# Router logits from the beta and output products of a delta-rule attention layer, with a new order of the calls in its loops

## The reference

```python
x = L0_attn_x                                   # (8, 512, 256)
x = x + attn(layernorm(x), ...)                 # 4 heads, dk 128, dv 64
x = x + ffn(layernorm(x), router_w, w1, w2)     # 8 experts, top 2, hidden 1024

# attn: q, k, v, g = x@Wq, x@Wk, x@Wv, x@Wg; beta = sigmoid(x@Wb); k normalised; q scaled
#   S_t = S_{t-1} + k_t (beta_t (v_t - k_t^T S_{t-1}))^T ;  o_t = q_t^T S_t
#   o = rms_norm(o) * norm_w * silu(g);  return o @ Wo
# ffn: probs = softmax(x @ router_w.T); the best two experts of each row
#   out = sum over the two of prob * (gelu(x @ w1[e].T) @ w2[e].T)
```

## Time and profile before

| What | Value |
|---|---|
| median of 3 runs | 910.33 us (907.74 to 911.69) |
| the profiled execution, its own time | 914.49 us |
| its span, first to last instruction | 912.7 us |
| TensorE busy | 850.3 us (93%) |
| TensorE weight loads busy | 669.4 us (73%) |
| VectorE busy | 625.5 us (69%) |
| ScalarE busy | 596.5 us (65%) |
| GpSimd busy | 439.3 us (48%) |
| granted TensorE clock, mean | 0.978 of full |

### The profile page before, as it was taken

The page is one execution under the profiler, slowest core; times in us unless marked ns, Lnnn a source line. Parts: engine busy times, 40 slices in busy tenths (PEclk is TensorE's granted clock), DMA queues, the critical chain, the costliest instruction groups (busy, mean ns, idle before and its releaser), DMA issues.

```text
span 912.7 us, 29508 instructions
## 1 busy us (share of the span) xinstructions
PE 850.3 (93%) x9870; PEld 669.4 (73%) x9871; DVE 625.5 (69%) x1832; ACT 596.5 (65%) x1645; POOL 439.3 (48%) x430
## 2 busy tenths in 40 slices
PE   3799999999999999999988979999999999999995
PEld 2578887788877888778876657777777777777773
DVE  4678898898988989888885755544455554455552
ACT  3478887888888888888766725444446544444551
POOL 2155554767677676676646543332223222222333
PEclk8999999999999999999997989999999999999998
DMA  6022222333233332332233252322233332223223
GB/s 225 2 71 66 82 65 77 95 95 106 84 95 99 90 107 83 97 99 82 84 107 88 72 118 48 48 48 48 43 48 66 50 50 46 46 46 46 47 36 34
DMA packets 50652, 67.14 MB, mean 74 GB/s; under 512 B 6464, under 2 KB 35008, under 8 KB 50528
## 3 DMA queue, kind: packets, MB, share of 16 engines
q1 hardware_dynamic: 36640, 46.46, 17.5%
q0 software_dynamic: 13344, 17.97, 11.5%
q10 hardware_dynamic: 544, 1.05, 0.3%
HBM read 41.84 MB, written 23.61 MB: 72 GB/s over the span
## 4 chain that ended last, share of the span: by engine, by line
PE 77%; issue 7%; ACT 4%; DVE 4%; POOL 4%; DMA 3%; SPq 0%; DVEq 0%; ACTq 0%; POOLq 0%
PE ps L1158 71%; DMA wst<-w 2%; PE ps L1247 2%; PE ps L1533 2%; ACT inverse_levels L789 1%; PE ps L1190 1%; PE ps L1413 1%; POOL kscale L616 1%; DVE inverse_levels L1815 1%; DMA wb_in<-wb 1%; POOL out L769 1%; POOL w_lo L665 0%; PE ps L1445 0%; ACT kq_wvg L844 0%; ACT Lh L789 0%
## 5 line engine op out<-in xcount | busy, mean ns | idle before, releaser
L789 ACT ACTIVATE inverse_levels<-ps 128x512 f16<-128x512 f32 (+1 forms) x324 | 163.0, 520 | 147.9 <-PE ps L1533 120.6
L769 POOL DMA_INDIRECT out<-inverse_levels,yidx x71 | 119.6, 1684 | 256.2 <-DVE inverse_levels L2273 194.6
L1158 PE MATMUL ps<-inverse_levels,w_hi 128*128 128x256 f16 (+1 forms) x1376 | 192.9, 255 | 1.9 <-issue 1.3
L2236 DVE SCALAR_TENSOR_TENSOR KpAT<-kq_wvg,inverse_levels 128x512 f16<-128x512 f32 (+1 forms) x144 | 98.5, 687 | 111.9 <-ACT inverse_levels L789 109.2
L1158 PE MATMUL ps<-inverse_levels,w_lo 128*128 128x256 f16 (+1 forms) x688 | 164.2, 255 | 0.0
L1158 PE MATMUL ps<-w_s,inverse_levels 128*128 x426 | 141.9, 379 | 6.5 <-issue 3.3
L1158 PEld LDWEIGHTS ps<-inverse_levels,w_hi 128*128 x1376 | 125.4, 98 | 15.7 <-issue 3.2
L1055 ACT ACTIVATE kq_wvg<-ps 128x512 f32<-128x512 f32 (+1 forms) x144 | 85.0, 590 | 67.0 <-PE ps L1158 51.1
L1158 PE MATMUL ps<-w_s,KpAT 128*128 x426 | 116.1, 273 | 1.0 <-issue 1.0
L789 ACT ACTIVATE inverse_levels<-kq_wvg 128x512 f16<-128x512 f32 (+1 forms) x144 | 89.8, 624 | 4.6
L1815 DVE CAST_PREDICATED inverse_levels<-mask_s,ps 128x256 f16<-128x256 int8 x192 | 82.1, 428 | 15.0 <-PE ps L1158 10.0
(11 more groups left out here) (239 smaller groups left out, 1920.7 us busy)
## 6 DMA issues: line engine op xcount, KB each, us to landing
wst<-w SPq DMA_DIRECT2D x58, 256.0 KB, 2.8
inverse_levels<-eye SPq DMA_DIRECT2D x35, 256.0 KB, 5.2
x_s<-x SPq DMA_DIRECT2D x32, 128.0 KB
out<-x_s SPq DMA_DIRECT2D x32, 128.0 KB, 1.7
x_s<-routed_rows SPq DMA_DIRECT2D x7, 260.0 KB
Lh<-routed_rows SPq DMA_DIRECT2D x7, 260.0 KB
Vp<-routed_rows SPq DMA_DIRECT2D x7, 260.0 KB
rowA<-routed_rows SPq DMA_DIRECT2D x7, 260.0 KB
```

What stands on the lines that cost most here:

```text
L769: pool.indirect_dma_start(out=out, out_offset=bass.IndirectOffsetOnAxis(ap=yidx[:, q, a:a + 1], axis=0), in_=yrow[:, q % 2, a, :], in_offs ...
L789: return act.activation(dst, src, ACT.Copy, scale=scale)
L1158: return pe.matmul(dst, lhsT, rhs, start=start, stop=stop, **kw)
L2236: dve.scalar_tensor_tensor(hlo[:, q % 2, two, 0:n], hf[:, m, :].rearrange("p (m n) -> p m n", m=2)[:, :, 0:n], H_SCALE, hhi[:, q % 2, two, ...
```

## The change

The second layernorm's router product is taken apart. With a router whose column means are removed, the logits of a row of x1 = x + attention are (x + attention) times router, times the row's own scale, since the subtracted mean drops out. So the 8 logits of x come from `beta_proj`, whose weight gets 8 more columns (4 to 12), times the first layernorm's deviation `sd1`; those of the attention part come from `wo_make`, whose weight gets 8 columns Wo times router (256 to 264). `x_s` is 264 wide, so `attention_residual` adds both in one instruction. `xn2T_make`, `xn2T_evac`, `logits_make` and `logits_copy` are gone.

```diff
-        wb_s = sb("wb_s", [P, 2, KC, H], fp16)
-        wo_s = sb("wo_s", [P, 2, KC, D], fp16)
+        wb_s = sb("wb_s", [P, 2, KC, H + E], fp16)
+        wo_s = sb("wo_s", [P, 2, KC, DX], fp16)
...
             def ln1_scale(n):
...
+                done(pool, s_xl, n - 4)
+                pool.tensor_scalar(sd1[:, n % 4:n % 4 + 1], mv[:, n % 2, 1:2], r[:, 0:1], 1.0 / A_SCALE, ALU.mult, ALU.mult).then_inc(s_sd, 1)
...
             def beta_exp(n):
...
                 act.activation(eb[:, :], p_beta, ACT.Exp, scale=-1.0 / A_SCALE).then_inc(s_eb, 1)
+                done(act, s_sd, n)
...
+                evac(x_s[:, n % XR, D:DX], p_xlogits, sd1[:, n % 4:n % 4 + 1]).then_inc(s_xl, 1)
...
-                    last = split_mm(p_beta, xnT_of, lambda part, k: wb_s[:, part, k, :], k)
+                    last = split_mm(p_beta_x, xnT_of, lambda part, k: wb_s[:, part, k, :], k)
...
+            def group_logits(n):
...
+                stt(logits[:, :, :], x_s[:, four, D:DX], 1.0, rs2[:, four, 0:1].broadcast_to([P, C, E]), ALU.mult, ALU.mult).then_inc(s_lgs, 1)
...
             act.dma_start(wvg_in, wvg.rearrange("(k p) n -> p k n", p=P)).then_inc(s_wload[2], 16)
+            act.dma_start(router_s[:, :, :], router.rearrange("(k p) n -> p k n", p=P)).then_inc(s_wb, 16)
             ln1(0)
-            act.wait_ge(s_wb, 16)
+            act.wait_ge(s_wb, 32)
+            act.wait_ge(s_rc, 2)
             evac(wb_s[:, 0, :, :], wb_in[:, :, :], A_SCALE)
```

The loops' order is new on all four engines. In TensorE's:

```diff
             for i in range(T + 3):
+                y_make(i - 3, 4)
                 gram(i - 2, 0)
                 gram(i - 2, 1)
+                x_make(i - 3, 4)
                 out_chunk(i - 4)
+                k_proj(i - 1, 0)
                 y_make(i - 3, 5)
-                k_proj(i - 1, 0)
-                xn2T_make(i - 5)
                 y_make(i - 2, 0)
                 state_make(i - 4)
                 x_make(i - 3, 5)
                 y_make(i - 2, 1)
-                logits_make(i - 5)
                 k_proj(i - 1, 1)
                 x_make(i - 2, 1)
+                q_proj(i - 1, 0)
+                oT_make(i - 4)
                 y_make(i - 3, 6)
-                oT_make(i - 4)
-                q_proj(i - 1, 0)
...
```

300 lines of the change are left out of this document (145 added, 155 removed).

## The result

The changed kernel takes **918.56 us**, median of 4 runs (917.15 to 918.62), beside 910.31 us for the kernel before on the same chip (907.74 to 911.69): a ratio of 1.0111 with a 95% interval of 1.0088 to 1.0135. It is 1.1% slower; 2.7% faster was forecast. The profiled execution of the changed kernel has an own time of 918.50 us (span 916.7) at a mean clock of 0.982.

What follows compares the result with a forecast made beforehand. TensorE's order was taken to bound the attention loop. 0.75 us off each of 31 tiles (23.2), +1.5 at the start and -3.0 at the end gave -24.7 us: 886 us from the 910.3 median, range 870 to 902.

Steps and rivals of the forecast that it cites:

- TensorE's order paces the loop: Attention loop: TensorE's own matmuls make 97.6% of the chain of waits over two tiles, so removing its work shortens tiles.
- Second part: K transposes to the next second `k_proj` half, 7.63 us: loses 0.65 us of router calls and 0.10 of waiting.
- First part: Second `k_proj` half to the k transposes, 6.64 us: no change, with 0.3 us either way.
- k chain: `k_square`, the k scale, `k_prime`, then the k transposes: removing matmuls cannot shorten it, only an earlier `k_square` would.
- The wait of 0.18 at `oT_make`: TensorE before `oT_make`: 0.18 us waiting for the logits copy goes, but counted as nothing, being under the k chain.
- both stay below 12.5 us a tile: ScalarE's and VectorE's load by busy shares: a tile of 13.5 us still leaves them 1 us, a thin cover.
- The rule against it: Reading by shares: VectorE at 88% and ScalarE at 86% exceed TensorE's weight loads at 80%, so removing TensorE work gives little.
- GpSimd at nothing: GpSimd's queue before the k scale: 1.6 us more work fits into 1.86 + 0.98 us of idle time, costing nothing.
- rival D: GpSimd's queue makes the k scale late: +0.95 us a tile, 938 us with the ends; chance 0.05.
- Start: Before the first tiles: router load and centring delay `wb_s` and k's weights; +1.5 us, between +0.5 and +4.
- End: Last tiles: router calls between expert products and their waits go; -3 us, between -1 and -6.
- Rival B: Attention loop: VectorE and ScalarE take over, waits before TensorE grow, 0.20 us a tile remains, 904.6 us; chance 0.20.

Runs made afterwards that it cites:

- e2_old_order: The changed kernel with all four engines' attention loops back in the old order, less the router calls, router columns kept; ratio 1.0084.
- e1: The changed kernel with six of VectorE's small routing calls moved to other places, nothing added or removed; ratio 1.0067.
- m1: e2_old_order with `nL` and its copy `Lh` made for the first three tiles only and reused for all others; ratio 1.0013.
- m2: The kernel before, router calls kept, with `nL` and `Lh` made for the first three tiles only and reused; ratio 0.9990.
- g2: e2_old_order with the first layernorm's row statistics on VectorE left out from the third tile on; ratio 1.0009.
- e3: The kernel before with the new order of calls on all four engines, its router calls kept on TensorE; ratio 1.0217.
- f5: f2 with the router's load on SyncE ahead of Wq, and its centring and `wb_s` later in the start; 904.71 us, ratio 0.9929.
- f2: e1 with ScalarE's `next_ln1` moved up behind `ln2`; ratio 1.0021.

## Why the prediction was wrong

**"TensorE's order paces the loop, and what is taken out of its line shortens the tile, until a chain through the other engines is longer."** This is the step that failed. TensorE's order didn't pace the loop alone: an ordinary tile takes 14.1 us in the kernel before and 14.1 in e2_old_order, where the removal alone gave nothing, and `oT_make` comes 8.75 and 8.71 us behind the k transposes. Something else was already as long; which chain it is stays open, since cutting links of the one that I read from the traces left the tile at 14.0 or more. Two things were misread. The 97.6% of the earlier trace rows came from a stretch where such a chain happens to be TensorE's; over 280 us it is 66%. And where TensorE shows no gap it doesn't follow that the next instruction could have started earlier: 0.22 us of `xn2T_make` stood exactly over a wait for `Lh`, and 0.44 us of the logits over waits for a mask and for `osq`. A matmul that starts without idle time may have become ready a moment before.

**Second part, -0.75 a tile.** It measured -0.24, and -0.51 once VectorE's held instructions were moved (e1). The router's 0.65 was the right size as work: m1 against m2 gives 0.66 in this part. The mistake was to count a shorter second part as a shorter tile.

**First part, "I take no change".** It measured +0.49, beyond the end of 0.3. I had named `k_square` as the head of the k chain, by adding up calls to 2.28 us; that number held. But the k scale needs two things: in the kernel before `k_square` ended 3.42 us behind the half and `beta_exp` 3.48, a tie. In the changed kernel they end at 3.62 and 3.93, and beta leads; in e2_old_order, with the calls in their old places, at 3.86 and 3.92. So both come later behind the half with either order, because the half comes earlier and they don't: the first part was taken for a fixed length from the half on, and it hangs on things that come before the half.

**The wait of 0.18 at `oT_make`.** "Waiting for the logits copy" was wrong: that copy ended at 300.30 + 0.21 = 300.51, `osq` by VectorE's timeline at 299.72 + 0.85 = 300.57, and `oT_make` followed at 300.72; the later one decides, and it stayed when the copy was gone. It was priced at nothing, but in e2_old_order the same wait is 0.29 us longer and the one for the mask of level 1 0.15, and together they take back the 0.44 of the logits.

**ScalarE and VectorE, "both stay below 12.5 us a tile".** VectorE measured 252.9 / 280 of 14.58, 13.2 us a tile; without the 0.85 of held instructions it would be 12.3. ScalarE measured 12.1. As cover the shares were useless: what mattered was when VectorE does its masks, and the held instructions, which no row of before priced. The Trainium skill (SBUF — State Buffer, "SBUF: two separate sides") says that VectorE and GpSimd share a port pair that is an exclusive lock, taken by a VectorE instruction with two SBUF inputs against a GpSimd one that reads SBUF, the later one blocking for the whole of the other. The trace agrees: 0.18 us became 1.03 beside a GpSimd instruction of 1.16, which had started first. I had not asked this rule which of the moved instructions would now meet `Ll` and `w_lo`.

**The rule against it** pointed the right way for the wrong reason: taking TensorE's work away did give little, but VectorE wasn't full. g2 relieved it by 0.83 us a tile and the ordinary tile kept its 14.1 us.

**GpSimd at nothing** was right; rival D falls, with 1.42 us idle before the k scale at 296.60. **Start**: +2.1 for +1.5, within 0.5 to 4. **End**: -7.7 for -3, beyond -6. Part of that is the clock: between 470 and 540 us the granted clock was at its lower level, 1.2 GHz, for 20.5 us in the kernel before and 17.1 in the changed one, which the prediction had set aside; 3.4 us less at half the clock can be worth 1.7 us at most. The rest isn't traced. **Rival B** (waits through VectorE and ScalarE, 0.20 us a tile left) was the nearest in kind, but it too kept the sign of a gain. The range ended at 902 since no case let the new order itself cost anything, though e3 shows that in the kernel before it costs 2.2%. My only slower rival was at GpSimd's queue.

## What to carry to other kernels

A chain of waits over two tiles is a sample; take it over many and see whether the same engine leads each time. Where several share it, price a removal at nothing until each of the calls behind the removed one is shown ready early enough. If a tile is cut in parts, ask of each part whether it is a length of its own or only the distance between two things that are set elsewhere. For every call that is taken out or moved, ask what the next one reads and when that was ready: the removed work may be what covered it. When an order moves VectorE's small two-input instructions, look which of GpSimd's long ones they now fall into; in a profile the loss shows as a duration, not as a wait.

## What the runs showed of the hardware

- VectorE instructions with two operands in SBUF, and the fp32 to int32 copy of `slot`, that start while GpSimd runs `Ll` or `w_lo` end within 0.1 us of its end: 184 ns became 1009, 196 became 1039, 215 became 881, 164 became 509 in the mean. One that starts 0.13 us before the GpSimd instruction isn't held. Instructions with one operand in PSUM, or with one operand in all, kept their durations there. Six routing calls in other places brought 0.34 us a tile back.
- Around the end of the attention half (440 to 540 us) the granted clock was at the lower of its two levels, 1.2 GHz, for 17 us (changed), 27 (f5), 33 (e1) and 34 (f2), though TensorE's calls of that stretch are the same in these four; it was 21 in the kernel before. No edit aimed at this, and what decides it stayed open; it makes the time behind the last k scale no evidence for edits of a few us.
- The six products of 12 columns are recorded with 0.29 us, as the six of 4 columns: the 8 columns of the logits cost nothing on TensorE, as forecast.
